# Moving the end of each token chunk of a feed-forward phase behind the first tiles of the next chunk

## The reference, cut to what matters

```python
Wq1 = _quantize(W1)                      # 2048 x 512, entries -1, 0, 1
Wq2 = _quantize(W2)                      # 512 x 2048
h = relu(einsum('bsd,fd->bsf', x, Wq1) + b1)
out = einsum('bsf,df->bsd', h, Wq2) + b2
y = _layernorm(x + out, axis=-1)         # (v - mean) / sqrt(var + 1e-5)
```

## Time and profile before

| what | value |
|---|---|
| median of 3 runs | 5414.19 us (5403.51 to 5415.39) |
| the profiled execution's own time | 5411.71 us |
| its span, first to last instruction | 5409.9 us |
| busy share of the span, PE / DVE / ACT / POOL | 85% / 75% / 66% / 59% |
| mean granted TensorE clock | 0.927 |

### The profile page before, as it was taken

One profiled execution on the slowest core, in us unless ns is written; L12 is line 12 of the kernel. 1 busy time (PEld: TensorE's weight loads), 2 busy tenths in 40 slices (PEclk: granted clock), 3 DMA queues, 4 the chain that ended last, 5 costly groups with the idle time before them and its releaser, 6 DMA issues. The chain is left out here.

```text
span 5409.9 us, 85208 instructions
## 1 busy us (share of the span) xinstructions
PE 4586.6 (85%) x23362; PEld 3179.0 (59%) x23362; DVE 4053.4 (75%) x4775; ACT 3570.6 (66%) x6726; POOL 3170.8 (59%) x2474
## 2 busy tenths in 40 slices
PE   5979788888989788889897988888787588888888
PEld 3656555555656565556565655556564477777776
DVE  5888888888889798988888888888886534444444
ACT  5878787878788778788887878787885122222222
POOL 4786868687878778787868686868785000000000
PEclk8999999999989899999898989999998799999999
DMA  2322333233333323232223332332232200000000
GB/s 93 96 89 90 99 92 100 88 102 98 98 103 90 99 89 101 88 101 94 96 90 97 93 96 91 103 97 98 87 93 68 79 31 31 31 31 31 31 31 16
DMA packets 233278, 436.73 MB, mean 81 GB/s; under 512 B 23872, under 2 KB 24000, under 8 KB 232320
## 3 DMA queue, kind: packets, MB, share of 16 engines
q1 hardware_dynamic: 232832, 431.55, 25.3%
HBM read 397.38 MB, written 34.08 MB: 80 GB/s over the span
## 5 line engine op out<-in xcount | busy, mean ns | idle before, releaser
L696 DVE TENSOR_TENSOR_SCAN h<-decay,carry,dbu 128x512 f32<-128x512 f32 x2048 | 2529.3, 1270 | 306.4 <-ACT decay L488 139.1
L445 POOL TENSOR_TENSOR dbu<-dtx,bb 128x1024 f32<-128x1024 f32 x1024 | 2461.5, 2404 | 5.5 <-issue 2.3
L488 ACT ACTIVATE decay<-dt,aneg 128x512 f32<-128x512 f32 x2048 | 1431.6, 701 | 698.5 <-DVE h L696 693.8
L871 PE MATMUL ht<-ident,h 128*128 128x128 f32 x8192 | 1338.9, 291 | 603.9 <-DVE h L696 451.6
L871 PEld LDWEIGHTS ht<-ident,h 128*128 128x128 f32 x8192 | 1011.5, 149 | 1329.3 <-issue 801.7
L502 ACT ACTIVATE ch<-ht,ct 128x256 f32<-128x256 f32 x3328 | 1404.2, 482 | 86.7 <-PE ht L871 85.0
L821 PE MATMUL gemm<-xt,win 128*128 128x512 f32 x2048 | 1074.4, 610 | 10.8 <-DMA win<-w_in 7.1
L876 PEld LDWEIGHTS y<-ident,ch 128*128 128x128 f32 x6656 | 790.2, 143 | 406.9 <-issue 363.1
L876 PE MATMUL y<-ident,ch 128*128 128x128 f32 x6656 | 892.2, 278 | 4.2 <-ACT ch L502 1.9
L419 POOL TENSOR_TENSOR carry<-h,ones_pair 128x2 f32<-128x2 f32 x1022 | 272.0, 266 | 862.9 <-DVE h L696 852.6
L1104 ACT ACTIVATE hr<-hidden_ps,b1c 128x512 f32<-128x512 f32 x256 | 174.3, 687 | 773.6 <-PE hidden_ps L1215 773.6
(11 more groups left out here) (90 smaller groups left out, 3588.5 us busy)
## 6 DMA issues: line engine op xcount, KB each, us to landing
bb<-b_rows SPq DMA_DIRECT2D x1024, 256.0 KB, 3.3
win<-w_in SPq DMA_DIRECT2D x256, 256.0 KB, 3.6
xt<-x_cm SPq DMA_DIRECT2D x16, 1024.0 KB, 6.6
xres<-x_tm SPq DMA_DIRECT2D x16, 1024.0 KB, 6.8
x<-xres SPq DMA_DIRECT2D x16, 1024.0 KB, 5.2
xr<-x SPq DMA_DIRECT2D x16, 1024.0 KB, 5.3
out<-xr SPq DMA_DIRECT2D x16, 1024.0 KB, 4.3
raw<-w SPq DMA_DIRECT2D x2, 4096.0 KB, 17.8
```

What stands on the lines that cost most here:

```text
L445: nc.gpsimd.tensor_tensor(dbu[:, u % 2, :, :], dtx[:, pair(q), :], bb[:, u % BB_RING:u % BB_RING + 1, :].to_broadcast([P, 2, TC]), ALU.mul ...
L488: nc.scalar.activation(DA[j][:, :], dt[:, c.par, i, :], ACT.Exp, scale=aneg[:, i, n:n + 1])\
L696: nc.vector.tensor_tensor_scan(h[:, H_SLOT[u], j, :], DA[j][:, :], dbu[:, u % 2, j, :], carry[:, c.par, n, i:i + 1], ALU.mult, ALU.add).th ...
L871: ins = nc.tensor.transpose(HT[k][:, tb % 2, j * P:(j + 1) * P], h[:, H_SLOT[u], j, tb * P:(tb + 1) * P], ident[:, :])
```

## The change

The end of a chunk is cut in pieces and put into the body of the next one. On VectorE the four residual additions come first, ahead of tile 0 of the next chunk. bn_stats follow after tiles 1 and 2 (two each), bn_aggr after tile 2, the normalisation after tiles 7 and 8 (two blocks each), and the bias additions go from tiles 8 to 11 to tiles 9 to 12. On ScalarE the Ln comes after the relu of tile 4, and the Exp after that of tile 6. The store waits for all four blocks' normalisation, which now signal one by one. `chunk_order` writes out the first and the last chunk, and loops over the 14 between. The end of chunk 15 stands after everything, as before. TensorE's code is the same.

```diff
+STATS_AFTER = {1: (0, 1), 2: (2, 3)}
+SUMS_AFTER, LN_AFTER, EXP_AFTER = 2, 4, 6
+APPLY_AFTER = {7: (0, 1), 8: (2, 3)}
+BIAS_AFTER = {9 + tb: tb for tb in range(TB)}
...
             def store(it, first, par):
-                sp.wait_ge(y_ready, it + 1)
+                sp.wait_ge(y_ready, it * TB + TB)
...
         def chunk_order(eng, body):
+            body(0, 0, 0, False)
             with eng.Fori(0, PAIRS - 1) as i:
-                for par in range(2):
-                    body(i, 2 * i + par, par, False)
-            body(PAIRS - 1, CHUNKS - 2, 0, False)
+                body(i, 2 * i + 1, 1, False)
+                body(i + 1, 2 * i + 2, 0, False)
             body(PAIRS - 1, CHUNKS - 1, 1, True)
...
             def chunk(i, it, par, last):
+                first = isinstance(it, int) and it == 0
                 for j in range(NJ):
...
+                    if j == LN_AFTER and not first:
+                        norm_ln(it)
+                    if j == EXP_AFTER and not first:
+                        norm_exp(it)
                 if not last:
                     split_hi(it + 1)
-                act.wait_ge(mv_ready, it + 1)
-                nc.scalar.activation(lnv[:, :], mv[:, :, 1], ACT.Ln, bias=epsln[:, :]).then_inc(lnv_ready, 1)
-                act.wait_ge(lnv_ready, it + 1)
-                nc.scalar.activation(rstd[:, :], lnv[:, :], ACT.Exp, scale=-0.5).then_inc(rstd_ready, 1)
             chunk_order(act, chunk)
+            norm_ln(CHUNKS)
+            norm_exp(CHUNKS)
...
             def chunk(i, it, par, last):
+                first = isinstance(it, int) and it == 0
+                if not first:
+                    residual(it, 1 - par)
                 for j in range(NJ):
...
+                    if not first:
+                        if j in STATS_AFTER:
+                            norm_stats(it, 1 - par, STATS_AFTER[j])
+                        if j == SUMS_AFTER:
+                            norm_sums(it)
+                        if j in APPLY_AFTER:
+                            norm_apply(it, 1 - par, APPLY_AFTER[j])
+                    if j in BIAS_AFTER:
+                        tb = BIAS_AFTER[j]
                         nc.vector.tensor_tensor(xr[:, par, tb, :], xr[:, par, tb, :], b2r[:, :], ALU.add)\
                             .then_inc(res_ready, 1)
```

More of the change, by code:

```diff
@@ L1096, in _, with norm_ln, norm_exp @@
             split_hi(0)
+            def norm_ln(done):
+                act.wait_ge(mv_ready, done)
+                nc.scalar.activation(lnv[:, :], mv[:, :, 1], ACT.Ln, bias=epsln[:, :]).then_inc(lnv_ready, 1)
+            def norm_exp(done):
+                act.wait_ge(lnv_ready, done)
+                nc.scalar.activation(rstd[:, :], lnv[:, :], ACT.Exp, scale=-0.5).then_inc(rstd_ready, 1)
             def chunk(i, it, par, last):
+                first = isinstance(it, int) and it == 0
                 for j in range(NJ):
@@ L1150, in _, with residual, norm_stats, norm_sums @@
             split_lo(0)
+            def residual(done, par):
+                dve.wait_ge(h_used, done * NJ)
+                dve.wait_ge(res_ready, done * TB)
+                for tb in range(TB):
+                    nc.vector.tensor_tensor(xr[:, par, tb, :], OP[tb][:, :], xr[:, par, tb, :], ALU.add).then_inc(added, 1)
+            def norm_stats(done, par, blocks):
+                for tb in blocks:
+                    dve.wait_ge(added, done * TB + tb + 1)
+                    nc.vector.bn_stats(stats[:, tb, :], xr[:, par, tb, :]).then_inc(stats_ready, 1)
+            def norm_sums(done):
+                dve.wait_ge(stats_ready, done * TB)
+                dve.sem_inc(stats_seen, 1)
+                for tb in range(TB):
+                    ins = nc.vector.bn_aggr(mv[:, tb, :], stats[:, tb, :])
+                ins.then_inc(mv_ready, 1)
+            def norm_apply(done, par, blocks):
+                dve.wait_ge(rstd_ready, done)
+                for tb in blocks:
+                    nc.vector.tensor_scalar(xr[:, par, tb, :], xr[:, par, tb, :], mv[:, tb, 0:1],
+                                            rstd[:, tb:tb + 1], ALU.subtract, ALU.mult).then_inc(y_ready, 1)
             def chunk(i, it, par, last):
+                first = isinstance(it, int) and it == 0
+                if not first:
+                    residual(it, 1 - par)
                 for j in range(NJ):
@@ L1160, in chunk @@
                                             ALU.subtract).then_inc(hlo_ready, 1)
-                    if j >= 8 and j < 8 + TB:
-                        tb = j - 8
+                    if not first:
[7 more added lines that the diff above has]
+                        tb = BIAS_AFTER[j]
                         nc.vector.tensor_tensor(xr[:, par, tb, :], xr[:, par, tb, :], b2r[:, :], ALU.add)\
@@ L1167, in chunk @@
                     split_lo(it + 1)
[L1168 to L1184, removed]
             chunk_order(dve, chunk)
+            residual(CHUNKS, 1)
+            norm_stats(CHUNKS, 1, range(TB))
+            norm_sums(CHUNKS)
+            norm_apply(CHUNKS, 1, range(TB))
         @block.tensor
```

## The result

The changed kernel takes 5277.66 us (median of 4 runs, 5271.46 to 5284.7) against 5412.06 us for the kernel before (4 runs): a ratio of 0.9747, 95% interval 0.973 to 0.9763. The profiled execution took 5271.46 us with a span of 5269.7.

What follows compares the result with a forecast made beforehand. Bound by the old chunk's end queued ahead of tile 0 at each seam, idling TensorE and slowing its clock. 5411.7 - 104.3 idle - 38.9 clock + 9.6 left over = 5278.1 us, range 5262 to 5298.

Steps and rivals of the forecast that it cites:

- What bounds it, and the two queues: At each seam, the old chunk's end stands ahead of tile 0 on VectorE and ScalarE; TensorE waits 101.8 us in all.
- Idle term: TensorE's idle time before down(0) at 15 seams, 6.98 us lost in the seam read: 104.3 us to be won back.
- Clock term: Matmuls after each seam's idle time run at granted clock 0.50: 38.9 us, all to be won back.
- What is left: Wait before down(0) after the change: 0.54 us plus restart loss, 0.64 per seam, 9.6 us over 15 seams.
- The sum: Profiled execution 5411.7 less idle and slow clock, plus the wait left over: 5278.1 us.
- Pieces inside the chunk at nothing: Moved pieces fit the idle gaps per tile, 2.59 us on VectorE and 3.06 on ScalarE, so cost nothing.
- the second cushion: Inside a chunk, a relu or cast may be late by 1.32 us without making TensorE wait.
- Store and load: Moved to mid-chunk; the load lands 12 us before the transposes that need it, so it costs nothing.
- rival 3: Slower: late store and load make TensorE wait before the transposes in 14 chunks; 5522 at four times today's length; chance 2%.
- Rival 1: The clock still falls at the seams, so 38.9 us stay lost: 5317; chance 5%.
- Rivals 2 and 4: 2: moved pieces overrun the cushions inside the chunk, 5338, chance 4%; 4: something unnamed holds down(0), 5412, chance 2%.

Runs made afterwards that it cites:

- e8: Kernel before, with only ScalarE's Ln, Exp and table loads moved behind the relus of tiles 0 and 1 of the next chunk: 5415.44 us, ratio 1.0003.
- e3: The change with bn_stats, bn_aggr, Ln and Exp back at the seam, so only normalisation and store move into the next chunk: 5392.24 us, ratio 0.9956.
- e4: Kernel before with 26 more matmuls of 128x512 ahead of down(0) in each chunk, into an unread PSUM bank: 5382.44 us, ratio 0.9949.
- e5: The change with all four normalisations and all four bias additions in one lump after tile 9: 5279.52 us, ratio 0.9755.
- e6: The change with the normalisations after tiles 11 and 12 instead of 7 and 8, so store and load start later: 5308.35 us, ratio 0.9796.
- e2: The change with two of the four bn_stats back at the seam, ahead of the first cast: 5293.72 us, ratio 0.9784.
- e1: The change with all four bn_stats and bn_aggr back at the seam, ahead of the first cast: 5349.85 us, ratio 0.9893.

## Why the prediction was right

- *What bounds it, and the two queues.* Right. e8 and e3 show the two halves of the chain separately: with ScalarE freed nothing changes, with the normalisation moved only 1.25 us per seam does.
- *Idle term, 104.3 us.* Right: 2.6 us of waits are left of 101.8.
- *Clock term, 38.9 us.* Right, and shown apart by e4: 32.7 against 32.8, of which 1.2 is luck, and 3.84 us for the 16 matmuls that took 6.44. The evidence it rested on was thinner than it said. The 0.54 in the earlier trace rows is idle time of the weight load (PEld). TensorE's matmuls stood 0.49 apart there, 0.26 more than the pitch, so the clock's staying up was known for half the wait that was forecast:

```profile
5393.25 0.39 PE L1226 MATMUL out_ps<-w2q,hlo 128*128 128x512 f32 x1
5393.74 0.50 PE L1226 MATMUL out_ps<-w2q,hhi 128*128 128x512 f32 x1
```

- *What is left, 0.64 per seam or 9.6 us.* The one term that was mis-sized. It measured 0.59 - 0.23 = 0.36 and 0.10 for the restart (0.33 to the second matmul), 0.46 per seam, 6.9 us. I had set a tile from inside a chunk on the seam: cast 1.35 after up's last start, down at 2.65. At the seam it was 1.15 and 2.46. The relu came at 0.43, not 0.52, and the cast started 0.03 after the relu's end, not 0.14. It is not for having stood in a queue, since tile 1's cast had 0.72 of idle time before it and came after 0.03 as well. In every chunk of the loop tiles 0 and 1 have these shorter times and the tiles behind them the longer ones. The code gives tiles from 2 on a second wait on both engines, for a buffer; the tile of the earlier trace rows is one of these. In the two chunks that are written out, tiles from 2 on have that wait too and still start after 0.43 and 0.03, so the slower tiles are those with a second wait inside the loop. No run isolates that. The residual additions, which I had ending 0.19 before the cast, end just when it starts.
- *The sum.* 143.2 - 6.9 = 136.3 against 136.6 in the phase, 0.3 of it from the phase's opening; the forecast was 133.6. The median lies 0.4 us from the number on record because the median of before lay 0.4 above its profiled execution and the runs of after some 6 above theirs; in the profiled executions the gain was 140.2, with 3.6 from the mixer. That closeness is partly luck.
- *Pieces inside the chunk at nothing.* Right; no new wait of TensorE appears, behind a moved piece the least idle time left is 1.44 on ScalarE and 0.75 on VectorE, where the forecast's figures give 2.59 - 1.76 = 0.83. e5 shows the second cushion exists.
- *Store and load, 12 us to spare.* 12.9 measured; e6 shows what lies behind it, so the mechanism of rival 3 is real and only its condition absent.
- *Rival 1, the clock doesn't come back.* Didn't occur: 1.00 over 888 us, and still 1.00 with 1.3 us idle at each seam (e2). The rule of the Trainium skill named there (TensorE: Matmul & The Clock Gate, A second HAM failure mode: psum-queue depth-cycling) is not what these rows show for waits of this length and number; the waits of 1.9 us in e6 are the shortest after which the clock fell. *Rivals 2 and 4* didn't occur either.

## What to carry to other kernels

Where an accumulator is drained between two rounds of matmuls, only what frees the accumulator has to stand ahead of the next round's first tile on the draining engines; the rest goes into the idle gaps of later tiles. Work out each queue's chain to the first tile with and without it, since freeing one of two engines in series may win nothing (e8). Count an idle time of TensorE of some microseconds twice, once as itself and once as the slow stretch behind it, and check what transfers are moved later by the same step against their deadline.

## What was not expected of the hardware

- More matmuls made the kernel faster: 26 idle-time matmuls per chunk took 32.7 us off the phase, as they kept the granted clock at 1.00 (e4).
- A wait of about 3 us at each seam gave a mixed picture: the clock fell before the first matmul, within the first 8 or, in one seam, not at all, and cost 22.9 us over 15 seams (e1), where 1.3 us cost no clock (e2) and 6.8 us cost 38.9. Waits of 1.9 to 2.0 us brought the clock down in six chunks of e6, while one of 2.8 didn't. The length of the wait alone does not decide it.
- How soon the cast follows its relu has two values in the changed kernel, whether VectorE was idle or not. Tiles 0 and 1 and both written-out chunks have about 0.03 us (60 of 256 casts), tiles from 2 on in the loop mostly 0.15 (187), and never less than 0.14. Inside a chunk this is hidden; at the seam it is over half of the 0.19 us by which the forecast's tile was too slow.
